# First chunk's token rows loaded as 96 and 4 partitions, small loads queued behind Wkv, and 36 transposes of the identity ahead of the first weight transposes

## The reference

```python
x = x + tanh(g_xattn) * xattn(layernorm(x), ctx, Wq, Wkv_expand, Wout)   # 16 heads of 32, causal, softmax
x = x + tanh(g_ffn)   * ffn(layernorm(x), router_w, gate_w, up_w, down_w) # best of 8 experts per token
# xattn: q = x @ Wq.T; k, v = split(ctx @ Wkv_expand.T); softmax(q k / sqrt(32)) v @ Wout.T
# x is (16, 100, 512), ctx is (16, 361, 128), of which the causal mask lets 100 rows count
```

## Time and profile before

| | us |
|---|---|
| median of 3 runs | 508.97 |
| the three runs | 506.72, 508.97, 513.75 |
| the profiled execution's own time | 510.96 |
| its span in the trace | 509.2 |
| PE busy in that span | 469.9 |
| DVE busy | 377.9 |

### The profile page before, as it was taken

The page is one execution under the profiler, slowest core; times in us unless marked ns, Lnnn a source line. Parts: engine busy times, 40 slices in busy tenths (PEclk is TensorE's granted clock), DMA queues, the critical chain, the costliest instruction groups (busy, mean ns, idle before and its releaser), DMA issues.

```text
span 509.2 us, 11847 instructions
## 1 busy us (share of the span) xinstructions
PE 469.9 (92%) x3892; PEld 396.8 (78%) x3892; DVE 377.9 (74%) x784; ACT 310.0 (61%) x877; POOL 170.2 (33%) x212
## 2 busy tenths in 40 slices
PE   0997999899989998988999999999999999999994
PEld 0885797679668965767888889888888988888882
DVE  2675767877797458875877888787788787887872
ACT  1557666684678366772567566575665756666661
POOL 4315323552654345455422213212232122320121
PEclk9995999999999989998999999999999999999999
DMA  7610120340032003925377976769767797677651
GB/s 189 183 35 3 40 77 2 98 159 21 1 97 80 16 5 98 281 68 184 87 202 213 293 238 210 227 203 286 237 208 224 225 269 232 214 233 242 190 168 32
DMA packets 59357, 77.26 MB, mean 152 GB/s; under 512 B 5552, under 2 KB 40974, under 8 KB 59324
## 3 DMA queue, kind: packets, MB, share of 16 engines
q1 hardware_dynamic: 54268, 66.92, 43.7%
q0 software_dynamic: 5056, 9.93, 6.6%
HBM read 67.76 MB, written 10.34 MB: 153 GB/s over the span
## 4 chain that ended last, share of the span: by engine, by line
PE 46%; DVE 16%; ACT 13%; DMA 11%; issue 10%; POOL 1%; SPq 1%; DVEq 0%; ACTq 0%; POOLq 0%
DMA staging<-in_L_ffn_gate_w 5%; ACT pr L774 5%; PE bank L1538 5%; PE bank L1539 4%; PE bank L1540 4%; PE gate_banks L1958 4%; PE up_banks L1958 4%; ACT gu_hi L723 4%; PE bank L1648 3%; ACT wq_hi L723 3%; DVE wq_lo L976 3%; PE gate_banks L1635 2%; DMA staging<-in_L_xattn_Wq 2%; DVE qT L1498 2%; PE up_banks L1960 2%
## 5 line engine op out<-in xcount | busy, mean ns | idle before, releaser
L976 DVE TENSOR_TENSOR gu_lo<-staging,gu_hi 128x1024 fp32r<-128x1024 f32 x64 | 78.1, 1222 | 18.0 <-ACT gu_hi L723 17.5
L1958 PE MATMUL gate_banks<-x_hl,gu_hi 128*128 128x448 f32 x256 | 83.5, 378 | 0.4 <-DVE x_hl L976 0.3
L1958 PE MATMUL up_banks<-x_hl,gu_hi 128*128 128x448 f32 x256 | 82.9, 376 | 0.0
L517 POOL TENSOR_TENSOR pn<-pr,inv 100x400 f32<-100x400 f32 x64 | 54.5, 854 | 62.6 <-DVE inv L1241 62.4
L723 ACT ACTIVATE gu_hi<-staging 128x1024 fp32r<-128x1024 f32 x64 | 67.4, 1055 | 4.5 <-DMA staging<-in_L_ffn_gate_w 4.1
L1960 PE MATMUL up_banks<-x_hl,gu_lo 128*128 128x224 f32 x256 | 68.1, 266 | 0.0
L1960 PE MATMUL gate_banks<-x_hl,gu_lo 128*128 128x224 f32 x256 | 68.1, 266 | 0.0
L723 ACT ACTIVATE wkv_hi<-qT 128x448 fp32r<-128x448 f32 x32 | 18.5, 578 | 69.7 <-DVE qT L1498 68.1
L1958 PEld LDWEIGHTS gate_banks<-x_hl,gu_hi 128*128 128x128 f32 x256 | 48.1, 188 | 6.5 <-issue 1.0
L774 ACT ACTIVATE pr<-gate_banks,nmx 100x100 f32<-100x100 f32 x128 | 42.2, 354 | 16.7 <-DVE nmx L1235 16.4
L1538 PE MATMUL bank<-wq_hi,wkv_hi 128*112 128x512 f32 x128 | 50.6, 395 | 1.9 <-DVE wkv_lo L976 1.8
(11 more groups left out here) (261 smaller groups left out, 1121.3 us busy)
## 6 DMA issues: line engine op xcount, KB each, us to landing
staging<-in_L_ffn_gate_w SPq DMA_DIRECT2D x32, 512.0 KB, 5.5
staging<-in_L_ffn_up_w SPq DMA_DIRECT2D x32, 512.0 KB, 6.6
staging<-in_L_ffn_down_w SPq DMA_DIRECT2D x32, 512.0 KB, 4.5
x_rows<-x SPq DMA_DIRECT2D x8, 800.0 KB
xt<-in_x SPq DMA_DIRECT2D x4, 800.0 KB
xr<-in_x SPq DMA_DIRECT2D x16, 200.0 KB
staging<-in_L_xattn_Wq SPq DMA_DIRECT2D x1, 1024.0 KB, 11.0
x<-in_L_xattn_Wout SPq DMA_DIRECT2D x1, 1024.0 KB, 8.9
```

The source lines that it names most:

```text
L517: nc.gpsimd.tensor_tensor(pn[0:S, n % DEEP], pr[0:S, n % 2], inv[0:S, n % HP].unsqueeze(2).to_broadcast([S, HP, S]), ALU.mult).then_inc(pr ...
L976: return nc.vector.tensor_tensor(dst, src, hi.bitcast(F32), ALU.subtract)
L1958: nc.tensor.matmul(pair[:, m, 0:2 * CAP], gu_hi[:, s, w, k, r], x_hl[:, :, k, 0:CAP], start=k == 0, stop=False, skip_group_check=True)
```

## The change

The first chunk's rows are loaded by two DMAs, partitions 0 to 95 and 96 to 99, and the semaphore `xt_loaded` counts 16 more. Wkv's load is issued right behind Wq's, ahead of the gates and the router. PE runs 36 transposes of the identity into the bank `misc_b` once the constants are there, ahead of its wait for Wq; nothing reads that bank before later work overwrites it.

```diff
-        xt_loaded = Signal(sem("xt_loaded"), 16)
+        xt_loaded = Signal(sem("xt_loaded"), 16, 16)
...
-            sp.dma_start(xt[0:S], x_chunk[0]).then_inc(xt_loaded.sem, 16)
+            for rows in (slice(0, 96), slice(96, S)):
+                sp.dma_start(xt[rows], x_chunk[0][rows]).then_inc(xt_loaded.sem, 16)
             sp.dma_start(ctx_t[0:S], ctx_chunk[0]).then_inc(ctx_loaded.sem, 16)
             sp.dma_start(wq_raw, Wq.rearrange("(o p) i -> p o i", p=P)).then_inc(wq_loaded, 16)
+            sp.dma_start(wkv_raw, Wkv.rearrange("(r p) l -> p r l", p=P)).then_inc(wkv_loaded, 16)
             sp.dma_start(gates[:, 0:1], ...).then_inc(small_loaded, 16)
             sp.dma_start(gates[:, 1:2], ...).then_inc(small_loaded, 16)
             sp.dma_start(router[:], router_w.rearrange("(k p) e -> p k e", p=P)).then_inc(small_loaded, 16)
-            sp.dma_start(wkv_raw, Wkv.rearrange("(r p) l -> p r l", p=P)).then_inc(wkv_loaded, 16)
...
+            def warm(n):
+                for _ in range(n):
+                    nc.tensor.transpose(misc_b[:, 0:P], ident[:], ident[:])
...
+            warm(36)
             for n in range(6):
                 turn_weights(n)
```

## The result

| | before | after |
|---|---|---|
| median | 509.34 us (22 runs) | 511.75 us (22 runs) |
| lowest to highest | 504.55 to 513.75 | 509.49 to 515.74 |
| profiled execution: time, span | 510.96, 509.2 | 510.22, 508.4 |

The ratio is 1.0067, 95% interval 1.0046 to 1.0088: a loss of some 3.4 us (the two medians themselves lie 2.4 apart), where a gain of 2.1 was forecast. By the bound of 2% that is no change.

The account below looks back on a forecast made before the run. PE was taken to be busy nearly throughout, so the gain was an earlier first keys matmul: norm 1.5 us earlier plus DVE's gaps gone, 2.1 us in all. Off the median of 508.97 that gave 506.9 us, range 503.3 to 510.8.

Parts of the forecast that it names:

- the fast pace: PE's start: Wq's transposes at 0.104 us each in place of 0.216; DVE can start 1.33 us after PE, not 1.75.
- DVE's gaps: DVE's six low halves before `c_lo`: 0.51 us of waiting for ACT and PE goes, leaving 3.60 of 4.11 us.
- the small loads: Gates and router, now behind Wkv's load: land at about 14, 2.5 us to spare before POOL wants them.
- the second chunk's statistics: DVE's work on the second chunk's rows: starts near 24.5 us, a sign to look for in the trace.
- A: Rival at PE's start: the 36 transposes stay slow, end at 13.5; 0.25 us slower, 509.2 us; chance 0.06.
- B: Rival in the first loads: the split spreads nothing, `xt` and Wq as before or 0.4 late; 508.5 us; chance 0.1.
- C: Rival at the start: small loads land late, POOL's copy and keys wait; 508.1 us; chance 0.06.
- The term for the loads: First loads: `xt` lands 1.5 us earlier, at about 7.5, and Wq 1.5 us earlier, at about 11.6.
- the gain at the start: First keys matmul: starts at 17.7 in place of 19.82, 2.1 us earlier.
- the lower bound that I gave for the rows: Load of `xt`: at least 1.1 us earlier, a second issue of 0.42 us taken off; upper bound 2.2.
- the price of the transposes: PE ahead of Wq: the 36 transposes take 5.3 us from about 5.75, end at 11.1, and cost nothing.
- D: Clock rival, first chunk's attention: one half-clock stretch more gives 510.5 us (chance 0.11), one less 503.3 (chance 0.07).

Follow-up runs that it names:

- after again: The changed kernel run once more, unaltered, for a second trace, against before: 511.00 us, ratio 1.0040 (1.0006 to 1.0074).
- after + 40: The changed kernel with 40 more increments of an unused semaphore, 112 instructions added in all, against before: 511.97 us, ratio 1.0081.
- before + 72: The kernel before with 72 increments of an unused semaphore at the head of PE's stream, against before: 511.90 us against 507.99, ratio 1.0056.

## Why the prediction was wrong

**What held.** The 36 warm PE up and end before Wq lands; Wq's transposes take the fast pace; DVE's gaps go (3.60 us for six low halves, as forecast); keys follow `c_lo` by 0.71 (forecast 0.7); the small loads are there at 14.2 (forecast 14) and nobody waits for them; the second chunk's statistics start at 24.77 (forecast 24.5). By rivals: A is out, for the transposes don't stay slow. Their starts lie 0.21 us apart for the first 22 or so and 0.11 for the rest; in the profile of after again, where the 36 take 5.53 us, the pace changes after 14. The Trainium skill ("TensorE: Matmul & The Clock Gate", Part 4: PE-mode transpose) has transposes not count toward a raised clock. These traces disagree with it. B is out by `xt`'s landings, and C by the router's.

**What was mis-sized.** The term for the loads: 1.5 us earlier. In the profile of after `xt` comes 0.89 and Wq 0.84 earlier, over all traces about 0.6 each (`xt` 8.75 on average without the split, 8.13 with it; Wq 12.96 and 12.4). That makes the gain at the start 1.4 us in place of 2.1, and is below the lower bound that I gave for the rows, 1.1. By itself it would have moved the forecast to 507.6.

**The step that failed** is the price of the transposes: "They cost nothing where they end before Wq lands, since PE has nothing else to do; behind them stand only the weights' transposes." Their time costs nothing, as I said. Their number does. With 72 instructions more in PE's stream a fetch of a 16 KB block comes at an earlier point of the program, and now falls on the chain last store, index load, gather. The price was put at nothing, and measured it was 0.64% for the 36 transposes alone and 0.56% for 72 instructions that do nothing. I listed the moved loads' queues with care and never asked what a longer stream of instructions does to the queue that no line of the kernel issues to. It was to be seen: the page's third section has a row for it, and two queries of the trace of before (when do its packets start; which small load is waited for near them) show a packet 8.3 us behind the index load and one as far ahead. Which of them 72 instructions would move, and how far, that trace doesn't tell: the one ahead stays, and of the one behind the runs show that 20 don't move it at all, 44 by 6 us and 72 by 8 to 9. But a loss of this kind belonged among the rivals.

**The rival on the other side**, D, was near in the amount and wrong in the place. It foresaw a loss of some 2 us over no change (510.5 against 508.97) through a stretch of half clock in the first chunk's attention, which falls there by itself. In that stretch after has less low clock than before, 3.4 us at 44.5; in all traces it lies between 3.4 and 13.7 us there, with no pattern by edit. The new low clock is at 232 us and has a cause, PE's wait for the gather. It is part of the price, not the mechanism: index load to gather cost 1.8 us more, up to the gathered transposes it is 3.4 with PE's wait, and the remaining 1.5 falls behind them, while the clock is low.

**What is shown and what is argued.** That the number of PE's instructions makes the loss is shown: 72 that do nothing bring it, 20 and 44 don't. 256, a whole block, don't by the trace alone, since the run's own time is 21 us longer for the increments. That it does so through the packet beside the small transfers rests on its place in fourteen traces, and on the packets that wait for its end: the last eight of the index load in after, after again and 36 transposes only (the fetch ends 3.57, 3.31 and 3.32 us behind the issue, they start from 3.56, 3.30 and 3.31 on), and the last two of the store in after + 40. In before + 72 the fetch ends at 2.59, when the load's last packets start in other traces too, and the delay is small. q8 isn't PE's alone by these traces: the packets 13 and 7 to 8 us ahead of the index load stay where they are, whatever PE has more, and only some of the 18 move. That the one that moves is PE's follows from its moving with PE's count. Why it lasts 2.1 to 3.7 us in the five collisions and 0.9 to 1.4 in its place in the others, the traces don't show. Where between 44 and 72 it tips wasn't tried, nor another way round the collision, such as the index load issued elsewhere. What the loads' edits are worth by themselves stays within the error: 0.9942 with them and 0.9961 without, on different chips.

## What to carry to other kernels

Instructions added to one engine's stream can have two prices: their time, and their number, which can shift later instruction fetches; here it was better to warm PE up with few wide matmuls rather than many small ones. When a change at the start makes a loss far from it, compare the two traces stage by stage between events that both have, and put the fetch packets of the DMA view beside the small transfers that others wait for; instructions that do nothing, in the same number, are the test. Where the difference sought is below 1%, two single profiles can point the wrong way: here the changed kernel's span was the shorter one.

## What the runs showed of the hardware

- A 16 KB instruction fetch that starts within 3.2 us ahead to 0.5 us behind the issue of a load of 0.9 KB, or on the small stores ahead of it, holds the chain up: the load landed after 3.2 to 4.7 us in place of 2.6 to 3.0, or the stores' end was seen after 4.7 us in place of 2.2 to 2.6. In four of the five traces the late packets begin within 0.02 us of the end of the fetch. With what hangs on it, that was 0.4 to 0.8% of this kernel's time, gains at the start already taken off.
- A semaphore increment in PE's stream took about 0.15 us: with 40 of them the transposes start at 8.16, with 184 at 30.15, and 21.99 / 144 = 0.153. The 72 (some 11 us, an estimate from this) ended before Wq had landed, and cost nothing at the start.
- The clock rose in the middle of a run of 128-column transposes in every trace that had them, and not at the same point: after some 14 to 26 of 36 in five traces (5.53 to 6.72 us for the 36).
- An issue on SyncE's queue sat for 4.75 us in after, at a load of 128 single values, behind 2.5 MB of loads; in before it sat 2.92 us at Wkv. The long issue isn't tied to the size of the load that is issued.
